# TensorE's transposes moved ahead of the gathering products, and its version products ahead of the next written rows, in a chain of rotations

## The reference

```python
def step(mat, t):                       # one rotation per edge, one after the other
    i, j, theta = t
    c = jnp.cos(theta); s = jnp.sin(theta)
    ri = mat[i]; rj = mat[j]
    mat = mat.at[i].set(c * ri - s * rj)
    mat = mat.at[j].set(s * ri + c * rj)
    return (mat, None)
mat, _ = jax.lax.scan(step, jnp.eye(256), (src, dst, edge_weight))
x = x + jnp.maximum(layernorm(x), 0) @ mat.T
```

## Time and profile before

| | us |
|---|---|
| median of 3 runs | 3405.53 (3404.73 to 3406.38) |
| the profiled execution | 3400.86 |
| its span on the core | 3399.1 |
| TensorE matmul busy in the span | 2549.1 (75%) |
| VectorE busy | 2318.5 (68%) |
| ScalarE busy | 1682.1 (49%) |
| GpSimd busy | 1550.8 (46%) |

### The profile page before, as it was taken

The page is one execution under the profiler, slowest core; times in us unless marked ns, Lnnn a source line. Parts: engine busy times, 40 slices in busy tenths (PEclk is TensorE's granted clock), DMA queues, the critical chain, the costliest instruction groups (busy, mean ns, idle before and its releaser), DMA issues. The chain is left out here.

```text
span 3399.1 us, 57507 instructions
## 1 busy us (share of the span) xinstructions
PE 2549.1 (75%) x13058; PEld 1931.2 (57%) x13059; DVE 2318.5 (68%) x5727; ACT 1682.1 (49%) x4017; POOL 1550.8 (46%) x1759
## 2 busy tenths in 40 slices
PE   2999998428899999999997348888781368888770
PEld 1888887313566666666665246666661256666660
DVE  4777777465577877777775637767678546666677
ACT  1656555201454554545553246666661256666651
POOL 1323332100444545544541067777760077777740
PEclk9999999769899999999998667878786767877885
DMA  2100000121565555555562145555541155555521
GB/s 72 17 9 8 10 8 8 42 58 61 168 162 155 154 154 153 161 147 158 156 161 54 31 140 138 138 137 138 138 111 31 51 157 144 141 140 144 139 76 38
DMA packets 186285, 348.91 MB, mean 103 GB/s; under 512 B 74085, under 2 KB 116478, under 8 KB 185951
## 3 DMA queue, kind: packets, MB, share of 16 engines
q0 software_dynamic: 83520, 249.39, 29.1%
q1 hardware_dynamic: 102685, 98.62, 10.2%
HBM read 325.45 MB, written 22.44 MB: 102 GB/s over the span
## 5 line engine op out<-in xcount | busy, mean ns | idle before, releaser
L1620 POOL DMA_INDIRECT t_rows<-table_h,t_istage x896 | 853.3, 952 | 266.0 <-issue 251.0
L1206 POOL DMA_INDIRECT b_rows<-table_kv,b_istage x448 | 480.2, 1072 | 391.1 <-PE b_pso L1343 268.2
L1707 PE MATMUL t_pso<-t_rows,t_hot 125*125 125x272 f32 (+1 forms) x1792 | 594.7, 487 | 71.6 <-DVE t_rows L1746 36.8
L1707 PEld LDWEIGHTS t_pso<-t_rows,t_hot 125*125 125x125 f32 x1792 | 399.8, 235 | 168.9 <-issue 73.0
L1268 ACT COPY b_asked<-b_psq 125x512 f32<-125x512 f32 x224 | 131.1, 585 | 471.1 <-PE b_psq L1307 471.1
L1746 DVE TENSOR_TENSOR t_rows<-t_rows,t_psm 125x1056 f32<-125x1056 f32 x224 | 276.6, 1235 | 32.9 <-issue 32.8
L1693 PE MATMUL t_pss<-node_scores,t_hot_t 125*125 x1792 | 271.5, 282 | 33.3 <-ACT t_hot_t L1651 30.9
L1693 PEld LDWEIGHTS t_pss<-node_scores,t_hot_t 125*125 125x125 f32 x1792 | 265.6, 228 | 48.5 <-issue 43.6
L1658 ACT ACTIVATE t_hot<-con_iota,g_dstl 125x125 f32<-125x125 f32 x896 | 280.3, 384 | 0.0
L1756 DVE TENSOR_TENSOR acc<-acc,t_pso 125x272 f32 (+1 forms) x448 | 192.3, 429 | 121.2 <-DVE acc L1756 70.6
L1307 PE MATMUL b_psq<-queries,b_hot_t 125*125 x896 | 235.1, 385 | 45.3 <-issue 26.7
(11 more groups left out here) (392 smaller groups left out, 5190.6 us busy)
## 6 DMA issues: line engine op xcount, KB each, us to landing
t_places<-targets SPq DMA_DIRECT2D x56, 488.3 KB
t_rows<-table_h,t_istage POOLq DMA_INDIRECT x896, 3.7
b_attr<-in_attr_t SPq DMA_DIRECT2D x224, 62.5 KB
b_places<-targets SPq DMA_DIRECT2D x28, 488.3 KB
b_rows<-table_kv,b_istage POOLq DMA_INDIRECT x448, 5.5
table_h<-d_stage SPq DMA_DIRECT2D x50, 132.8 KB
t_flag<-flags SPq DMA_DIRECT2D x56, 62.5 KB
table_kv<-d_moved SPq DMA_DIRECT2D x25, 128.9 KB
```

What stands on the lines that cost most here:

```text
L1206: pool.indirect_dma_start(out=rows[:, h, s, :], out_offset=None, in_=table, in_offset=bass.IndirectOffsetOnAxis(ap=istage[:, h, s:s + 1], ...
L1620: pool.indirect_dma_start(out=rows[:, r, s, :], out_offset=None, in_=table, in_offset=bass.IndirectOffsetOnAxis(ap=istage[:, r, s:s + 1], ...
L1707: mm = pe.matmul(ps_o[b % 2][0:P, at:at + mw], hot[:, r, b * G + u, :], rows[0:P, r, b * G + u, 0:mw], start=u % PAIR == 0, stop=u % PAIR ...
```

## The change

In TensorE's list the two transposes leave the head of a step and are issued for the next step, in front of the current step's wait for Z and its gathering products. A first pair stands ahead of the loop. Within k = 0 the version products for u = 0 come before `written` and no longer behind it. VectorE gets one more wait ahead of writing Z: Z of the step before may be overwritten only once the gathering products that read it are done (`fset`), which the transposes' place behind those products saw to before.

```diff
@@ VectorE, body
                         fields(c, j, q)
                         for u in U:
                             dve.wait_ge(evac[u], n * STAGES + 1)
+                        if started(i, p):
+                            dve.wait_ge(fset, n)
                         dve.tensor_tensor(Z[:], upper[:], ident[:].unsqueeze(1).to_broadcast([128, UB, 128]), ALU.add).then_inc(zset, 1)
@@ TensorE
+                def turn(n, p):
+                    pe.wait_ge(built, n + 1)
+                    for u in U:
+                        mm = pe.transpose(ps_w[p][:, 256 + u * 128:384 + u * 128], lower[:, p, u, :], ident[:])
+                    mm.then_inc(uset, 1)
+
                 def body(i):
                     for p in range(2):
                         n = 2 * i + p
-                        pe.wait_ge(built, n + 1)
-                        for u in U:
-                            mm = pe.transpose(ps_w[p][:, 256 + u * 128:384 + u * 128], lower[:, p, u, :], ident[:])
-                        mm.then_inc(uset, 1)
                         for k in range(LEVELS):
                             if k < LEVELS - 1:
                                 raise_level(n, p, k)
@@
                             if k:
                                 extend(n, p, k)
-                            if k == 0:
-                                written(*following(i, p))
                             if started(i, p) and k in VERSIONS_AFTER:
                                 u = VERSIONS_AFTER.index(k)
                                 versions(n - 1, u, fresh=opening(i) and u == 0)
+                            if k == 0:
+                                written(*following(i, p))
                             if started(i, p) and k in ROWS_AFTER:
                                 rows_of(n - 1, 1 - p, ROWS_AFTER.index(k))
+                        turn(n + 1, 1 - p)
                         pe.wait_ge(zset, (n + 1) * LEVELS)
                         pe.wait_ge(gated, n + 1)
@@
                 pe.wait_ge(minit, 1)
+                turn(0, 0)
                 peeled(pe, more + 1, body)
```

## The result

| us | before | after |
|---|---|---|
| median of 5 runs each | 3404.73 (3399.11 to 3406.38) | 3375.93 (3372.77 to 3383.72) |
| the profiled execution | 3400.86 | 3375.93 |
| its span | 3399.1 | 3374.2 |

The ratio is 0.9921, with a 95% interval of 0.9905 to 0.9937, so the runs by themselves say 21 to 32 us less. The forecast was 3378.7. In the two profiles the change is 24.9 us.

A forecast was written before the change was run, and what follows sets the result against it. Bound: TensorE and VectorE handing over in turn, 15.81 us per step. 30 periods at 0.87 plus 0.74 in step 1 make 26.8, taking 3400.86 to 3374.1; plus 4.67 gives 3378.7 us, range 3368 to 3390 (8 in 10).

The forecast's parts named there:

- The ring: TensorE from fields to `keep` (3.84 us), VectorE back to fields (11.94), 0.05 between: 15.83 us, the period.
- The size: Versions leaving TensorE's stretch between fields and `keep`: 0.87 us less per step, bounds 0.77 and 0.98.
- the sum: Whole phase: 30 periods at 0.87 us make 26.1, with step 1's 0.74 us 26.8 us in all.
- The median: Whole kernel: median of the runs stands 4.67 us above the profiled execution, so 3374.1 becomes 3378.7 us.
- The transposes as cover: TensorE before the fields: moving the transposes frees 0.74 us, making room for the versions and adding no gain beyond it.
- The spare: TensorE before the fields: path of 2.91 us against VectorE's 3.42 + 0.05, leaving 0.56 us.
- The waits: VectorE's added wait before L485 comes 2.2 us early, cost 0; `ft` is ready 0.4 us before TensorE needs it.
- the slower rival: Versions ahead of the row products start late because `ft` or the M update is late: 3421 us, chance 0.04.
- The larger gain: TensorE is the real bound and its pauses go: 1.4 us per step, 45 us, 3361 us, chance 0.05.

The follow-up runs named there:

- transposes alone: Changed kernel with the versions put back behind the row products, so only the transposes move against the kernel before: ratio 0.999.
- versions alone: Kernel before with only the versions put ahead of the row products, transposes left at the head of the step: ratio 0.9932.
- counts: Changed kernel with the counts of written rows also put ahead of the row products, behind the versions: 3354.85 us, ratio 0.9842 against the kernel before.
- the last kernel: Counts-ahead kernel with transposes and half of the last `rows_of` ahead of Z's last extension, other half behind: 3351.58 us, ratio 0.9828 against the kernel before.

## Why the prediction was right

- **The ring.** The step on which all rests, that only TensorE's work between the fields and `keep` counts, held in each test: work taken away outside the ring gave 0.00 us per step (transposes alone), work taken out of it gave 0.77 (versions alone), other work taken out of it gave 0.74 (counts), and fields that came sooner gave 0.53.
- **The size.** 0.87 per step forecast, 0.86 measured. The whole way from the first gathering products to the last was 580.93 - 91.47 = 489.46 us before and is 554.62 - 91.91 = 462.71, 26.75 less; the sum said 26.8. The gap that the Trainium skill gives for an isolated matmul (TensorE: Matmul & The Clock Gate, Back-to-back issue gap), 109 ns for 256 columns, would have halved this. The traces disagree with it for these fp32 products, each of which the profile shows as two matmul instructions: one instruction took 0.87/4 = 218 ns before, and again 218 ns in the kernel after, where the versions of step 1 start at 93.80 and the row products at 94.67.
- **The median.** The last term of the forecast, the 4.67 us by which the median stood above the profiled execution before, came to nothing: after the change the profiled execution is the median. The profiled execution itself fell 1.9 us less than the sum said. That the two misses partly cancel and leave 2.8 us is luck.
- **The transposes as cover.** They fitted into the gap and added nothing. Their worth was put too high, though. The prediction said that the two edits need each other; the versions alone brought 0.77 of the 0.86. It gave 0.69 for them, since it left out that row products without a wait ahead are 0.11 us shorter, which its own rows showed as 0.44 and 0.55.
- **The spare.** 0.56 us forecast, 0.65 measured. The mis-sized term is the four squarings, 0.99 behind a pause and 0.90 without one (257.38 - 256.48). Step 1 gained 0.84 where 0.74 was said, for the same reason: from its gathering products to the next squaring there were 95.51 - 91.47 = 4.04 us and are 95.11 - 91.91 = 3.20.
- **The waits.** VectorE's new one is hidden: the period with it and the old order is 15.81. `ft` was in time (256.68, versions at 257.38 behind the squarings), so the slower rival had no footing. The granted clock was 1.00 from 90 to 555 us.
- **A rival's sum.** The larger gain was priced at some 1.4 us per step and 3361, but its two terms, 0.74 and 0.87, make 1.61, some 50 us and 3356. It still lay outside the range, and transposes alone, with a gain of 0.00, refuted its mechanism.

The two profiled executions differ by 24.9 us, 1.8 less than the way between the gathering products. Of this, 0.44 lie ahead of the first of them (91.91 against 91.47; the nine profiles have 91.5 to 92.5 there) and 1.4 behind the last. The rest of the phase takes the same time in both (9.23 us up to its last transposes, from 580.93 to 590.16 and from 554.62 to 563.85), so the 1.4 are in later phases, whose code is the same. The runs of one kernel differ by more than that; the medians differ by 28.8.

## What to carry to other kernels

When two engines wait for each other in turn, neither busy share tells the bound. Follow the hand-overs once around and add them up until they give the period; only work between a hand-over received and the next one given is worth moving. An engine's wait for its partner is room for work: put there what now stands just behind the hand-over, and look how large the room is before and after. When the room is full, as after the counts were moved, the engine's own way around, with its other pauses, becomes the bound, and the next gain has to come from those.

## What was not expected of the hardware

A group of matmuls is shorter when nothing is waited for in front of it: four of the row products took 0.44 us from start to start, and 0.55 behind a wait; the four pairs of squarings 0.90 and 0.99. Each of these two waits that went away thus gave some 0.1 us on top of the wait. It isn't the wait alone, as the row products took 0.53 behind the one-column counts with no wait shown (in the last kernel they start at 262.85 and the squarings at 263.38). The weight loads (PEld) of the row products, the first two from the kernel after and the third from the last kernel, suggest what it is:

```profile
94.45 0.63 PEld L608 LDWEIGHTS r_psw<-con_ident,r_fld 128*128 128x128 f32 x4
258.90 0.52 PEld L608 LDWEIGHTS r_psw<-con_ident,r_fld 128*128 128x128 f32 x4 [0.90 <-DVE r_fld L388]
```

```profile
262.82 0.53 PEld L608 LDWEIGHTS r_psw<-con_ident,r_fld 128*128 128x128 f32 x4
```

Where the group took 0.44 us, its first weights began to load 0.22 us ahead of its first product (94.45 for 94.67), under the products of the group before. Behind the wait load and product have the same start, 258.90, and behind the counts the load is only 0.03 ahead. So the 0.1 us look like a weight load that is no longer hidden. This is read from the rows; no run was made for it.
